# Cross-attention and ternary feed-forward on one core: GpSimd makes the output scales, the value half of the key/value weight is transposed later, and the work around the seam and at the end stands in another order

## The reference, cut to what matters

```python
# x: (16, 56, 256), ctx_512: (16, 1500, 64); 16 heads of 16
def xattn(q, latent_kv, Wq, Wkv_expand, Wout):
    qp = q @ Wq.T
    k, v = split(latent_kv @ Wkv_expand.T)
    scores = einsum("bhqd,bhkd->bhqk", qh, kh) / 4
    scores = where(tril((56, 1500)), scores, min)    # causal: 56 keys of 1500 are left
    out = einsum("bhqk,bhkd->bhqd", softmax(scores), vh)
    return out @ Wout.T

def qlinear(x, w):                       # ternary weight, 8-bit token
    ws = mean(abs(w)) + 1e-5;  wq = clip(round(w / ws), -1, 1)
    xs = max(abs(x)) / 127 + 1e-5;  xq = clip(round(x / xs), -128, 127)
    return (xq @ wq.T) * xs * ws

x = x + xattn(layernorm(x), ctx, Wq, Wkv_expand, Wout)
y = layernorm(x)
x = x + qlinear(silu(qlinear(y, w_gate)) * qlinear(y, w_up), w_down)   # 256 -> 1024 -> 256
```

## Time and profile before

| | |
|---|---|
| time, median of 3 runs | 91.86 us (91.49 to 92.05) |
| time of the profiled execution | 91.38 us |
| its span | 89.6 us, so 1.8 us lie around the span |
| PE busy | 79.8 us (89%) |
| DVE busy | 71.2 us (79%) |
| ACT busy | 54.2 us (60%) |
| POOL busy | 50.5 us (56%) |
| granted TensorE clock | 1.00 |

### The profile page before, as it was taken

One profiled execution on the slowest core, in us unless ns is written; L12 is line 12 of the kernel. 1 busy time (PEld: TensorE's weight loads), 2 busy tenths in 40 slices (PEclk: granted clock), 3 DMA queues, 4 the chain that ended last, 5 costly groups with the idle time before them and its releaser, 6 DMA issues.

```text
span 89.6 us, 2477 instructions
## 1 busy us (share of the span) xinstructions
PE 79.8 (89%) x908; PEld 56.7 (63%) x908; DVE 71.2 (79%) x176; ACT 54.2 (60%) x96; POOL 50.5 (56%) x106
## 2 busy tenths in 40 slices
PE   4999999999999999999999994999764979998580
PEld 1367655788787887879778774745232646765360
DVE  4738988894695898989489994668999999999650
ACT  0610345699179859825969642978382869886400
POOL 5630378639708974669479626080648646559610
PEclk9999999999999999999999999999999999999999
DMA  1788999810000000028009090000000000101133
GB/s 27 215 269 258 320 377 368 334 48 0 7 0 11 4 0 0 0 58 187 0 13 228 19 215 0 7 0 0 0 0 0 0 0 4 59 11 55 59 117 117
DMA packets 11747, 7.59 MB, mean 85 GB/s; under 512 B 6552, under 2 KB 11480, under 8 KB 11736
## 3 DMA queue, kind: packets, MB, share of 16 engines
q1 hardware_dynamic: 11068, 6.93, 26.1%
q10 hardware_dynamic: 668, 0.51, 1.9%
HBM read 4.95 MB, written 0.92 MB: 65 GB/s over the span
## 4 chain that ended last, share of the span: by engine, by line
PE 69%; DVE 16%; ACT 6%; issue 3%; POOL 2%; POOLq 1%; DVEq 0%; ACTq 0%
PE bank L898 35%; PE sc L898 20%; PE bank L1029 7%; DVE h_sb L810 5%; DVE amax L817 4%; PE bank L1053 3%; ACT tern L596 2%; PE bank L1110 2%; ACT v_wide L569 1%; DVE shifted L724 1%; POOLq L145 1%; PE bank L965 1%; ACT pT L384 1%; PE bank L957 1%; ACT wf_sb L616 1%
## 5 line engine op out<-in xcount | busy, mean ns | idle before, releaser
L898 PE MATMUL sc<-wT,xqT 128*128 128x512 bf16 x56 | 13.9, 380 | 3.0 <-DVE h_sb L810 3.0
L307 POOL TENSOR_SCALAR wf_sb<-h_sb,r_tok 128x512 f32<-128x512 f32 x13 | 9.1, 715 | 10.0 <-DVE r_tok L831 10.0
L616 ACT ACTIVATE wf_sb<-sc,s_out 128x512 f32<-128x512 f32 x14 | 9.7, 689 | 5.5 <-PE sc L898 2.7
L810 DVE SCALAR_TENSOR_TENSOR h_sb<-sc,s_out,wf_sb 128x512 f32<-128x512 f32 x14 | 9.9, 740 | 1.1 <-ACT wf_sb L616 1.1
L457 POOL TENSOR_SCALAR veps<-mv 128x1 f32<-128x1 f32 x13 | 2.5, 190 | 14.3 <-DVE mv L678 9.4
L898 PEld LDWEIGHTS sc<-wT,xqT 128*128 128x128 bf16 x56 | 4.9, 98 | 8.9 <-DVE h_sb L810 5.0
L715 DVE TENSOR_REDUCE mx<-sc 128x16 f32<-128x896 f32 x8 | 8.7, 1088 | 2.1 <-PE sc L898 2.0
L898 PEld LDWEIGHTS bank<-v_wide,pT 128*64 128x64 f32 x256 | 8.1, 138 | 2.4 <-issue 2.2
L898 PE MATMUL bank<-v_wide,pT 128*64 128x34 f32 x256 | 9.0, 225 | 0.1
L817 DVE TENSOR_REDUCE amax<-h_sb 128x1 f32<-128x1024 f32 x7 | 8.5, 1220 | 0.2
L724 DVE TENSOR_TENSOR shifted<-sc,mx 128x896 f32<-128x896 f32 x8 | 8.7, 1083 | 0.1
(11 more groups left out here) (109 smaller groups left out, 167.6 us busy)
## 6 DMA issues: line engine op xcount, KB each, us to landing
wf_sb<-in_L_ffn_w_gate_dram SPq DMA_DIRECT2D x1, 1024.0 KB, 8.9
wf_sb<-in_L_ffn_w_up_dram SPq DMA_DIRECT2D x1, 1024.0 KB, 10.9
wf_sb<-in_L_ffn_w_down_dram SPq DMA_DIRECT2D x1, 1024.0 KB, 13.0
out_dram<-k_wide SPq DMA_DIRECT2D x7, 128.0 KB, 1.7
x_sb<-in_x_dram SPq DMA_DIRECT2D x1, 512.0 KB, 6.5
wq_sb<-in_L_xattn_Wq_dram ACTq DMA_DIRECT2D x1, 256.0 KB, 3.6
x_sb<-in_x_dram SPq DMA_DIRECT2D x1, 256.0 KB, 3.5
wo_sb<-in_L_xattn_Wout_dram SPq DMA_DIRECT2D x1, 256.0 KB, 9.1
```

Source lines behind the costliest of these rows:

```text
L307: ops.tensor_scalar(h_int[:, t % 2, c, :], h_sb[:, t % 3, GC * c:GC * c + GC], r_tok[:, 1, t:t + 1], CODED, ALU.mult, ALU.add).then_inc(hi ...
L616: nc.scalar.activation(g_sb[:, t % 2, GC * c:GC * c + GC], SC[:, j % 4, :], ACT.Silu, scale=s_out[:, 0, t:t + 1]).then_inc(silu_ready, 1)
L810: nc.vector.scalar_tensor_tensor(h_sb[:, t % 3, cols], SC[:, j % 4, :], s_out[:, 1, t:t + 1], g_sb[:, t % 2, cols], ALU.mult, ALU.mult).th ...
L898: return nc.tensor.matmul(*a, **k)
```

## The change: what it does

- `gate_up_scales` and the down scale (new `down_scales`) are GpSimd's: the first behind `round_tokens`, the second behind the two roundings of a slot. VectorE has neither.
- `wkvT` 1 moves from second place to behind the second transpose of the context. There are three products of zeros behind `wkvT` 0 and none elsewhere, where there had been three and one. The copies of `wkvT` 0, `ctxT` 0 and `wqT` go to ScalarE.
- In slot 0 `xT` 1 comes first. The layer norm of tile 6 moves from slot 2 to slot 0. VectorE takes four more copies (`k` of the second half, `q` 2-4, `q` 4-6, `xT` 6). The widenings are one in each of the slots 0 to 3.
- The magnitudes of w_up are summed by ScalarE in slot 1, not by VectorE in slot 3. The first rounding of weights goes from slot 2 to slot 3, and the signs stand three in slot 5 and three in slot 6.
- `q` 6-8 moves from slot 5 to slot 3.
- In slot 8 `tr` of the last pair comes ahead of `aT` of pair 6, on TensorE and on ScalarE, and `op` of tile 5 moves to slot 9.
- In slot 16 `dn` of tile 5 comes ahead of `ht` of tile 6. Of the last tile GpSimd rounds the first half and VectorE the second, not the other way round. The sum with x of tile 4 goes to ScalarE and GpSimd.

```diff
-OP_SLOTS = [3, 4, 5, 6, 7, 8, 10]
+OP_SLOTS = [3, 4, 5, 6, 7, 9, 10]
 AMAX_SLOTS = [4, 5, 6, 7, 8, 10, 11]
 XQ_SLOTS = [5, 6, 7, 9, 11, 12, 13]
-LN1_SLOTS = {-1: [1, 2, 3, 4], 0: [5], 1: [], 2: [6], 3: []}
-ABS_SLOTS = {(0, 'scalar'): [0], (3, 'scalar'): [2], (3, 'vector'): [1]}
+LN1_SLOTS = {-1: [1, 2, 3, 4], 0: [5, 6], 1: [], 2: [], 3: []}
+ABS_SLOTS = {(0, 'scalar'): [0], (1, 'scalar'): [1], (3, 'scalar'): [2]}
 MEAN_SLOTS = [1, 4, 4]
-ROUND_SLOTS = [2, 3, 4, 4, 5, 5]
-SIGN_SLOTS = [3, 4, 5, 5, 6, 6]
+ROUND_SLOTS = [3, 3, 4, 4, 5, 5]
+SIGN_SLOTS = [5, 5, 5, 6, 6, 6]
 WARM_PRODUCTS = 6
-WARM_MORE = {('ctxT', 0): 1, ('wkvT', 1): 3}
+WARM_MORE = {('wkvT', 0): 3}
...
-MISC_JOBS = {-1: [('wkvT', 0), ('wkvT', 1), ('ctxT', 0), ('xT', 0), ('wqT', 0), ('k', 0, (0, 1), (0, 1)), ('ctxT', 1), ('q', 0, 1),
+MISC_JOBS = {-1: [('wkvT', 0), ('ctxT', 0), ('xT', 0), ('wqT', 0), ('k', 0, (0, 1), (0, 1)), ('ctxT', 1), ('wkvT', 1), ('q', 0, 1),
       ('k', 1, (0, 4), (1,))],
- 0: [('k', 0, (1, 4), (0,)), ('xT', 1), ('k', 0, (1, 4), (1,)), ('q', 1, 2), ('k', 1, (0, 4), (0,)), ('v', 0), ('v', 2),
+ 0: [('xT', 1), ('k', 0, (1, 4), (0,)), ('k', 0, (1, 4), (1,)), ('q', 1, 2), ('k', 1, (0, 4), (0,)), ('v', 0), ('v', 2),
      ('xT', 3), ('xT', 2)],
...
- 3: [('xT', 4), ('woT', 0), ('xT', 6), ('q', 4, 6)],
+ 3: [('xT', 4), ('woT', 0), ('xT', 6), ('q', 4, 6), ('q', 6, 8)],
  4: [],
- 5: [('q', 6, 8)]}
+ 5: []}
...
-VECTOR_READS = [('k', 0, (0, 1), (0, 1)), ('k', 0, (1, 4), (1,)), ('xT', 4), ('v', 2), ('wkvT', 0), ('xT', 0), ('xT', 1), ('ctxT', 0),
- ('wqT', 0), ('q', 1, 2)]
+VECTOR_READS = [('k', 0, (0, 1), (0, 1)), ('k', 0, (1, 4), (1,)), ('xT', 4), ('v', 2), ('xT', 1), ('q', 1, 2), ('xT', 0),
+ ('k', 1, (0, 4), (0,)), ('q', 2, 4), ('q', 4, 6), ('xT', 6)]
...
-SUB_BEHIND = {0: 3, 1: 4, 2: 4, 3: 4}
+AT_BEHIND = [8]
+SUB_BEHIND = {0: 4, 1: 1, 2: 9, 3: 4}
...
-WIDENINGS = {0: [], 1: [(1, 1, 1)], 2: [(1, 1, 0)], 3: [(1, 0, 1), (1, 0, 0)]}
+WIDENINGS = {0: [(1, 0, 0)], 1: [(1, 1, 1)], 2: [(1, 0, 1)], 3: [(1, 1, 0)]}
...
- ('gpsimd', 'gpsimd'), ('vector', 'gpsimd')]
+ ('gpsimd', 'gpsimd'), ('gpsimd', 'vector')]
...
-FINISHER = ['gpsimd', 'gpsimd', 'gpsimd', 'gpsimd', 'vector', 'vector', 'vector']
+FINISHER = ['gpsimd', 'gpsimd', 'gpsimd', 'gpsimd', 'gpsimd', 'vector', 'vector']
...
+            def gate_up_scales(s):
+                if s in AMAX_AT:
+                    t = AMAX_AT[s]
+                    pool.wait_ge(y_scale_ready, t + 1)
+                    wait_read(pool, ("mean", 0), ("mean", 1))
+                    nc.gpsimd.tensor_tensor(s_out[:, 0:2, t], w_scale[:, 0:2], s_tok[:, 0, t:t + 1].to_broadcast([P, 2]),
+                                            ALU.mult).then_inc(gu_scale_ready, 1)
+
+            def down_scales(s):
+                t = s - GU0
+                if 0 <= t < NT:
+                    pool.wait_ge(h_scale_ready, t + 1)
+                    wait_read(pool, ("mean", 2))
+                    nc.gpsimd.tensor_tensor(s_out[:, 2, t:t + 1], s_tok[:, 1, t:t + 1], w_scale[:, 2:3],
+                                            ALU.mult).then_inc(dn_scale_ready, 1)
...
             for s in range(NT_SLOT0, SLOTS):
                 round_tokens(s)
+                gate_up_scales(s)
                 second_variance(s)
                 second_rstd(s)
                 second_layer_norm(s)
                 round_gated(s, 0)
                 round_gated(s, 1)
+                down_scales(s)
                 add_residual(s)
...
             for s in range(NT_SLOT0, SLOTS):
-                if s == NT_SLOT0:
+                if s == NT_SLOT0 and s not in AT_BEHIND:
                     transpose_attention(s - 2)
                 transpose_scores(s)
+                if s == NT_SLOT0 and s in AT_BEHIND:
+                    transpose_attention(s - 2)
                 misc_products(s)
...
-                transpose_gated(s)
-                down_projection(s)
+                if s == HT0 + NT - 1:
+                    down_projection(s)
+                    transpose_gated(s)
+                else:
+                    transpose_gated(s)
+                    down_projection(s)
```

More of the change, by code:

```diff
@@ L138, in xattn_ffn @@
         at_last = [("aT", NP - 1)] if s == NP else []
-        for job in at_jobs + tr_jobs + misc[s] + op_jobs + pv_jobs + at_last + ht_jobs + dn_jobs:
+        first_jobs = tr_jobs + at_jobs if s in AT_BEHIND else at_jobs + tr_jobs
+        last_jobs = dn_jobs + ht_jobs if s == HT0 + NT - 1 else ht_jobs + dn_jobs
+        for job in first_jobs + misc[s] + op_jobs + pv_jobs + at_last + last_jobs:
             misc_no[job] = len(misc_no)
@@ L632, in _ @@
             for s in range(NT_SLOT0):
-                read_attention(s - 2)
+                if s not in AT_BEHIND:
+                    read_attention(s - 2)
                 exponentials(s)
+                if s in AT_BEHIND:
+                    read_attention(s - 2)
                 read_misc_banks(s, 0, None)
@@ L785, in invert_token_scales @@
                     nc.vector.reciprocal(r_tok[:, 0, t:t + 1], s_tok[:, 0, t:t + 1]).then_inc(y_ready, 1)
-            def gate_up_scales(s):
-                if s in AMAX_AT:
-                    t = AMAX_AT[s]
-                    dve.wait_ge(y_scale_ready, t + 1)
-                    wait_read(dve, ("mean", 0), ("mean", 1))
-                    nc.vector.tensor_tensor(s_out[:, 0:2, t], w_scale[:, 0:2], s_tok[:, 0, t:t + 1].to_broadcast([P, 2]),
-                                            ALU.mult).then_inc(gu_scale_ready, 1)
             def invert_weight_scale(s):
@@ L831, in invert_gated_scales @@
                     nc.vector.reciprocal(r_tok[:, 1, t:t + 1], s_tok[:, 1, t:t + 1]).then_inc(r_ready, 1)
-                    wait_read(dve, ("mean", 2))
-                    nc.vector.tensor_tensor(s_out[:, 2, t:t + 1], s_tok[:, 1, t:t + 1], w_scale[:, 2:3],
-                                            ALU.mult).then_inc(dn_scale_ready, 1)
             def round_gated(s, c):
@@ L868, in _ @@
                 second_stats(s)
-                gate_up_scales(s)
                 second_moments(s)
@@ L1129, in _ @@
                 scores(s)
-                transpose_attention(s - 2)
+                if s not in AT_BEHIND:
+                    transpose_attention(s - 2)
                 transpose_scores(s)
+                if s in AT_BEHIND:
+                    transpose_attention(s - 2)
                 misc_products(s)
```

## The result

The changed kernel takes 91.07 us, the median of 20 runs (90.65 to 91.78); the kernel before, run beside it 20 times, takes 91.56. The ratio is 0.9933, with a 95% interval of 0.9911 to 0.9955: some 0.6 us faster, less than 1%. The profiled execution of the changed kernel took 91.62 us with a span of 89.5, so as a pair the two profiled executions (91.38 and a span of 89.6 before) show almost nothing. There are two reasons, and both are read before anything else.

The account below looks back on a forecast made before the run. TensorE was taken to bound the kernel up to the seam, VectorE behind it. Terms -0.1 + 0.6 - 1.6 + 1.0 - 0.7 - 0.1 = -0.9 us gave 91.0 against the 91.86 median, range 89.9 to 92.2.

Parts of the forecast that it names:

- Start, -0.1: Ahead of and in slots 0 and 1: one zero product gone, 0.2 of 0.3 given back; -0.1 us (-0.3 to +0.4).
- give-back: Slots 0 and 1: tile 5's norm some 0.3 later, TensorE idles some 0.4; 0.2 of the start's 0.3 us lost.
- Signs, +0.6: Slots 5 and 6, three signs each: ScalarE late, TensorE loses 0.2 in slot 6, 0.4 in slot 7; +0.6 us (0 to +1.3).
- TensorE's cushion: Slot 6: slack of 0.25 to 0.3 us before ScalarE's lateness delays TensorE's `op` and `pv`.
- rival (a): Slots with signs and start: ScalarE keeps pace, the start keeps its 0.3; sum -1.6 to -1.7, 90.2 us; chance 0.22.
- Seam, -1.6: Slot 8: transposes of scores fill TensorE's wait for `attn`, `pv` 7 and SiLU start earlier; -1.6 us (-1.0 to -1.8).
- `op` in slot 9, +1.0: Slot 9: tile 5's sum with x and moments now stand between two `h_sb` on VectorE; +1.0 us (+0.8 to +1.1).
- Scales, -0.7: Behind the seam: scales leave VectorE's chain, down scale 0.4, the other 0.3; -0.7 us (-0.8 to -0.1).
- (d): Scales on GpSimd: at 0.55 each, VectorE waits instead of computing; sum -0.3, 91.6 us; chance 0.12.
- End, -0.1: Last tiles: `dn` 5 fills TensorE's wait, `ht` 6 waits for GpSimd's rounding, last product at 86.9; -0.1 us (-0.4 to +0.3).
- Rival (c): Last rounding of weights: GpSimd over 2 us behind 49.1, holding ScalarE's last sign and TensorE; 92.9 us; chance 0.10.
- Rival (b): Signs and seam: gains cancel, signs cost 1.3 and the seam gives 1.3; sum about 0, 91.8 us; chance 0.14.

Follow-up runs that it names:

- the long execution: Profiled execution of the changed kernel without zero products, with K's copy on ScalarE and the old end; one of three runs at 95.36 to 95.67 us.
- the first experiment: Changed kernel with order, zero products and copy engines ahead of slot 0 as before: 91.41 us, ratio 0.9941; it also lists other kernels' doubling moments.

## Why the prediction came out right, step by step

The time was right: 91.0 said, 91.07 measured. The sum was -0.9, and the median span, in the batch that has it for both, fell by 0.9. But the time fell by some 0.6, and among the terms one was wrong outright and three were mis-sized.

**Start, -0.1: -0.25, right in kind.** One product of zeros gone, 0.2 and not 0.32, since I had the length of one product and not the step to the next; nothing for V's half turned later; and a give-back of 0.15 in slot 1 by the norm of tile 5, which comes as named and goes when K's copy is taken off VectorE. Not seen was what `xT` 1 ahead of K's products does to them, 0.2 less. Together -0.25.

**Signs, +0.6: the step failed.** They cost nothing that shows: with the signs spread over three slots, slot 6 is the same 4.54. The step that broke is the sum of 1.58 and 3.2 us of ScalarE's work put against 4.40: the 1.58 had waiting in it. From the copy of `aT` to the exponentials took 0.44 in the earlier trace rows, and 0.28 back to back (47.12 to 47.40). The whole is 1.42 to the first sign and 3.12 from there to the next slot's copy (51.66), 4.54 and not 4.85. ScalarE had no idle time ahead of `aT`, as I had said, but its lateness didn't grow, and TensorE's cushion took what there was. The 0.14 by which slot 6 did grow is mainly, as I read the rows, the round of 4.56 through VectorE and GpSimd, laid bare because `q` 6-8 left slot 5; with `q` 6-8 put back the round no longer holds slot 6, but only 0.05 of the 0.14 came back, so it isn't the only limit there. I had said of that move that it moves "no end". So of rival (a) the half on ScalarE was true, and the half on the start was not.

**Seam, -1.6: right for SiLU, 0.3 too high behind it.** SiLU's first half is 1.50 earlier behind `pv` 6, and what I had named as late next, ScalarE's table load and copy, is what it stands behind. The second `h_sb` is 6.84 behind `pv` 6 against 8.14, only 1.30 earlier: between its two halves ScalarE now waits for `aT` of pair 7. Its copy of that stands at 58.87 with 0.23 idle ahead of it, and the second half of SiLU at 59.36.

**`op` in slot 9, +1.0: right,** by 1.00 in the rows. That it is no mishap but the price of the seam is what the kernel with it alone shows.

**Scales, -0.7: right in kind, -0.5 in size.** From the first `h_sb` of one tile to that of the next the way fell by 0.31 and 0.12 in slots 9 to 11, which is the 0.3 that I had said and a down scale in each, but by 0.05 in all three behind them, where I had counted 0.06 each. A link of 0.06 in the chain is the way from one start to the next; the next instruction would have waited 0.04 of it anyway. GpSimd takes 0.19 to 0.20 for one, so (d) is out. The Trainium skill (GPSIMD Engine Reference, Engine selection) puts such a product on GpSimd at about twice VectorE's time; the rows have 0.19 against 0.14. Around the span they cost 0.1 that I had no term for.

**End, -0.1: +0.07 in the trace, and 0.25 around the span.** In the changed kernel:

```profile
83.48 0.48 DVE L320 TENSOR_SCALAR wf_sb<-h_sb,r_tok 128x512 f32<-128x512 f32 x1
...
83.55 0.98 POOL L320 TENSOR_SCALAR wf_sb<-h_sb,r_tok 128x512 f32<-128x512 f32 x1 [0.79 <-DVE r_tok L860]
...
84.67 0.61 PE L1134 MATMUL bank<-ident_h,wf_sb 128*128 128x128 f16 x8
...
85.09 0.60 ACT L601 ACTIVATE hT<-bank 128x512 bf16<-128x512 f16 x1 [1.30 <-PE bank L1134]
...
85.84 1.03 PE L922 MATMUL bank<-wdT,hT 128*128 128x256 bf16 x8 [0.56 <-ACT hT L601]
```

The transposes wait for the slower of the two roundings. GpSimd's is first in TensorE's order now, so all eight transposes start at 84.67; with the old order four start when VectorE's half is done, ahead of it. That much I had counted: the transposes start 1.19 behind VectorE's last rounding (1.18 said) and ScalarE's copy 0.42 behind them (0.45 said). What the sum left out comes after. The eight products start 0.15 behind the end of that copy, not at it, and take 1.03, not half of 1.91. Together that is 0.2, and it turns -0.1 into +0.07. GpSimd's rounding takes 0.98 beside VectorE's in both kernels; 0.98 was in the sum.

Rival (c) didn't come about: the last rounding of weights ended at 49.82, 0.7 behind my 49.1 and ahead of the last sign. Rival (b) named the seam at 1.3, which is what came, and the signs at 1.3, which did not.

So -0.25 + 0.14 - 1.3 + 1.0 - 0.5 + 0.07 = -0.84 in the span, and +0.35 around it. The sum of the prediction was near by luck, because +0.6 for signs that cost nothing covered gains taken too high elsewhere (0.3 of the seam, 0.2 of the scales), and the forecast of the time because its 0.9 was taken from a first median, 91.86, that lay 0.3 above that of the 20 runs.

## What to carry to other kernels

Count every closed round of a slot against the slot, through several engines too, not only the work of the engine that you add to: 4.54 through VectorE and GpSimd against TensorE's 4.40 was in the trace of before, hidden by one long slot ahead of it. Before you call an instruction's time in the chain its price, look at how soon the next one starts where it is absent; and take an engine's minimal round from rows where its instructions follow each other without waiting. And set the span's change beside the time's: an edit can cost outside the trace, and a profiled pair can differ by where the start fell.

## What the runs showed of the hardware

**Time around the span.** It is 1.72 to 1.74 us in kernels with the old end and the scales on VectorE, 1.84 to 1.87 with the scales on GpSimd, and 2.07 to 2.11 with the new end as well, as medians of 6 to 29 runs each. The runs show which edits bring it; why, the trace doesn't show, and I didn't find out. In the new end GpSimd has two sums behind its last rounding instead of one; whether that is the reason was not tested.

**The rate of TensorE's products at the start.** Two rates are seen, some 0.45 and 0.22 to 0.25 us for a product of 128x512. They fit the two levels of the clock, 1.2 and 2.4 GHz, and the change comes between 4.55 and 7.20 us from the span's start, elsewhere in each of the eleven ordinary executions listed in the first experiment. The granted clock in the profile's rows is 1.00 over the whole start, in the long execution too, shown here by a window of that one (us, then the busy time of PE, PEld, DVE, ACT and POOL, the granted clock, the DMA share, GB/s):

```profile
10.00:14.00 4.00, 4.00 (x24) 2.84 (x22) 2.23 (x10) 1.06 (x3) 2.50 (x8) 1.00 1.06 360
```

So in this stretch the column doesn't tell the rate, and the durations do. The records behind the column do tell it: in the packed trace of every other profiled execution a record of full clock begins where the products become twice as fast (6.73 us in the changed kernel, 5.06 in the kernel before), and in the long one there is no clock record at all. The 1.00 stands where nothing is recorded. The Trainium skill (TensorE: Matmul & The Clock Gate, Seeing it yourself) warns that the recorded clock events were observed to be unreliable. Here the records agree with the products wherever there are any, and it is the column that misleads. What decides between an ordinary and a long start is not settled: the long one followed a wait of 0.26 for the context, but another execution had a wait of 0.49 at the same place and stayed ordinary.

**The granted clock at the seam.** In the profiled execution of the kernel with `op` alone, TensorE is busy for 0.39 to 0.85 of each us from 54 to 58, and then the column does fall:

```profile
57.00:58.00 1.00, 0.43 (x9) 0.46 (x10) 0.49 (x4) 0.98 (x2) 0.35 (x1) 0.77 0.00 0
58.00:59.00 1.00, 1.00 (x25) 1.00 (x23) 0.00 (x0) 0.93 (x2) 0.14 (x1) 0.50 0.05 16
```

At 0.50, that is 1.2 GHz, `pv` takes 1.93 instead of 1.13. That execution took 94.33, and the six lay between 92.51 and 94.57. A wait at the seam was thus followed by more than its length in this execution, and perhaps in the one of 94.57, which has the same mean clock (0.982). The changed kernel, with the shorter wait, showed none of it at the seam in its two profiled executions.

**Two roundings beside each other.** Who starts second is the slow one. In the changed kernel VectorE is first (83.48, 0.48 us) and GpSimd takes 0.98. In the kernel with the old start GpSimd is first:

```profile
84.09 0.70 POOL L321 TENSOR_SCALAR wf_sb<-h_sb,r_tok 128x512 f32<-128x512 f32 x1 [0.80 <-DVE r_tok L861]
84.27 0.79 DVE L321 TENSOR_SCALAR wf_sb<-h_sb,r_tok 128x512 f32<-128x512 f32 x1 [0.28 <-DVE r_tok L861]
```

The Trainium skill (SBUF — State Buffer, Who interferes with whom) has that rule for GpSimd and a VectorE instruction in a mode that uses both pairs of ports, as a `tensor_scalar` can be: whoever issues first gets the shared pair, and the other one is blocked. That VectorE's rounding runs in such a mode no run here shows. The trace agrees in the order; in size GpSimd loses 0.28 us to 0.41 of overlap, and VectorE 0.31 to 0.52.
